# First attention with merged window triangles: half as many probabilities, both heads normalised by VectorE in one multiplication

## What is computed

```python
q = rms_norm(einsum('btd,ndh->btnh', x, q_kernel), q_norm_scale)      # 16 heads of 128
k, v = einsum('bsd,ckdh->cbskh', x, kv_kernel); k = rms_norm(k, k_norm_scale)   # 8 key/value heads
q, k = apply_rope(q, positions), apply_rope(k, positions)
mask = (j <= i) & (i - j < 128)                                       # WINDOW = 128
logits = einsum('btkgh,bskh->bkgts', q * ATTN_SCALE, k)
probs = softmax(where(mask, logits, min))
out = einsum('btnh,nhd->btd', einsum('bkgts,bskh->btkgh', probs, v), out_kernel)
```

## Time and profile before

| | us |
|---|---|
| median of 3 runs | 1585.34 (1585.33 to 1596.49) |
| the profiled execution | 1583.67 |
| its span, first to last instruction | 1581.4 |

### The profile page before, as it was taken

The page is one execution under the profiler, slowest core; times in us unless marked ns, Lnnn a source line. Parts: engine busy times, 40 slices in busy tenths (PEclk is TensorE's granted clock), DMA queues, the critical chain, the costliest instruction groups (busy, mean ns, idle before and its releaser), DMA issues.

```text
span 1581.4 us, 24555 instructions
## 1 busy us (share of the span) xinstructions
PE 1452.6 (92%) x7806; PEld 1104.6 (70%) x7806; DVE 1112.8 (70%) x2356; ACT 810.5 (51%) x1983; POOL 334.4 (21%) x448
## 2 busy tenths in 40 slices
PE   3699999999999999799999999999849898989898
PEld 2589989988998899667777777777624344444376
DVE  5699899989998999377555455455437676767554
ACT  2466676666766767444332332332215464646566
POOL 3364454444444544000000000000012020201000
PEclk9899999999999999899999999999957899999999
DMA  4210000000000000233000000000052232222001
GB/s 130 67 41 1 2 1 1 1 3 1 1 2 1 1 1 1 67 90 90 21 1 0 0 0 0 0 0 0 1 204 65 70 91 70 90 70 90 1 14 40
DMA packets 30796, 52.75 MB, mean 33 GB/s; under 512 B 4480, under 2 KB 12544, under 8 KB 30304
## 3 DMA queue, kind: packets, MB, share of 16 engines
q1 hardware_dynamic: 30288, 50.63, 10.3%
q0 software_dynamic: 400, 0.78, 0.3%
HBM read 37.49 MB, written 14.68 MB: 33 GB/s over the span
## 4 chain that ended last, share of the span: by engine, by line
PE 83%; DVE 7%; ACT 4%; issue 3%; DMA 2%; POOL 0%; SPq 0%; DVEq 0%; ACTq 0%; POOLq 0%
PE ps L1216 16%; PE ps L1218 15%; PE ps L1217 15%; PE ps L1254 6%; PE ps L1300 6%; PE ps L1491 4%; PE ps L1530 4%; PE ps L1331 3%; PE ps L1281 2%; PE ps L1618 2%; PE ps L1504 2%; PE ps L1367 1%; PE ps L1636 1%; PE ps L1292 1%; PE ps L1516 1%
## 5 line engine op out<-in xcount | busy, mean ns | idle before, releaser
L806 DVE TENSOR_REDUCE nm<-ps 128x1 f32<-128x512 f32 x256 | 167.6, 684 | 101.8 <-PE ps L1491 101.7
L1138 ACT ACTIVATE pT<-ps 128x512 f32<-128x512 f32 x256 | 145.9, 597 | 140.0 <-PE ps L1504 137.6
L1216 PE MATMUL ps<-xnT_lo,w1moe_hi 128*128 128x512 f32 x400 | 177.0, 443 | 4.7 <-DVE w2moe_lo L764 4.5
L399 POOL TENSOR_TENSOR ln_rs<-ln_ve,minus_half 128x4 f32<-128x4 f32 x12 | 13.6, 1131 | 775.2 <-DVE ln_ve L496 775.2
L1068 ACT ACTIVATE moe_act_hi<-sg 128x512 fp32r<-128x512 f32 x100 | 63.3, 633 | 191.0 <-DVE sg L741 191.0
L1217 PE MATMUL ps<-xnT_hi,w1moe_lo 128*128 128x512 f32 x400 | 160.5, 401 | 0.0
L1218 PE MATMUL ps<-xnT_hi,w1moe_hi 128*128 128x512 f32 x400 | 159.9, 400 | 0.0
L1216 PE MATMUL ps<-wqkv_lo,xnT_hi 128*128 128x512 f32 x256 | 128.1, 500 | 25.5 <-DVE wqkv_lo L549 25.5
L998 ACT ACTIVATE rope<-ps 128x384 f32<-128x384 f32 x128 | 62.9, 491 | 156.4 <-PE ps L1218 155.4
L731 DVE TENSOR_TENSOR sg<-ps,sg 128x512 f32<-128x512 f32 x100 | 69.0, 690 | 95.5 <-ACT sg L1088 95.3
L424 POOL TENSOR_TENSOR rope<-rope 128x384 f32<-128x384 f32 x128 | 131.7, 1029 | 0.0
(11 more groups left out here) (205 smaller groups left out, 3688.7 us busy)
## 6 DMA issues: line engine op xcount, KB each, us to landing
copies<-qk_hi SPq DMA_DIRECT2D x32, 256.0 KB
yT<-in_w1moe SPq DMA_DIRECT2D x25, 256.0 KB, 2.6
qst<-copies SPq DMA_DIRECT2D x64, 96.0 KB, 2.2
kst<-copies SPq DMA_DIRECT2D x64, 96.0 KB, 2.3
x_res<-in_wqkv SPq DMA_DIRECT2D x8, 512.0 KB, 3.7
copies<-qk_lo SPq DMA_DIRECT2D x16, 256.0 KB
w_in<-in_w2moe SPq DMA_DIRECT2D x25, 128.0 KB, 2.7
x_res<-in_wo SPq DMA_DIRECT2D x4, 512.0 KB, 3.8
```

What stands on the lines that cost most here:

```text
L806: V.tensor_reduce(nm1[:, n % 2, t, col:col + 1], ps[:, 1 + s1_slot(p), :], AX.X, ALU.max, negate=True).then_inc(s1_max, 1)
L1138: A(pT1[:, u % 2, 2 * (m % 2) + h, c, :], ps[:, 4 + e % 2, :], ACT.Exp, scale=SCALE1).then_inc(p1_ready, 1)
L1216: MM(out, left[0], right[1], start=first, stop=False)
```

## The change

For the groups that see two tiles (96 of 128 steps):

- the scores of both tiles are written side by side in PSUM as before, but with no mask matmul; VectorE then copies the older tile's scores over the newer tile's where j > i (`copy_predicated` with an int32 mask `older`, 2 x 128 columns in PSUM, with a one-element memset ahead of it). Maximum, exponentials, normalisation and transposes then work on 2 x 128 columns instead of 2 x 256. Groups of tile 0 keep a mask matmul (`causal`, 256 columns).
- the transposed probabilities (2 x 128 columns) are parted again by GpSimd with two `affine_select`s over 256 elements each: zeros in one copy where the newer tile holds, in the other where the older holds (`parted`, 4 slots). The two products with v take these. In the hardware loop a one-element addition (`idle`) stands ahead of them. `part_probT` runs ahead of L420 in GpSimd's step, for the group of seven steps ago.

For all groups: VectorE normalises both heads in one multiplication with the two reciprocals broadcast (2 x 128 columns); ScalarE's L1014 is gone. On VectorE the order is now reciprocal, merge, normalisation, low part of the output, maximum. The product with v, the output's parts and the output projection come one step later (n - 9, n - 10; LAST_LAG = 10).

At the start: chunk 1 is loaded ahead of the tables, ScalarE and VectorE split two chunks before the first step and then chunk n + 2 ahead of step n; VectorE makes the rope tables of tile 0 only, GpSimd those of the tiles 1 to 3 behind its steps 0 to 2, and its splits of wo come one step sooner (behind steps 6 to 9). `prob` now lies in the memory of yT, so the first exponential also waits for the tables.

The diff, cut to its core:

```diff
-KV_RING, PROB_RING = 2 * GROUPS, 4
-LAST_LAG = 9
+OLDER_STEPS = STEPS - GROUPS
+K_RING, V_RING, PROB_RING, PART_RING = 2 * GROUPS, 4 * GROUPS, 4, 4
+LAST_LAG = 10
...
-        window = sb("window", [P, 2, 2, P], BF16, part_a)
+        idle = sb("idle", [P, 1], where=part_a)
+        causal = sb("causal", [P, 2, P], BF16, part_a)
+        older = sb("older", [P, 2, P], I32, part_a)
...
-        prob = sb("prob", [P, PROB_RING, 2, 2 * P], where=part_a)
+        prob = yT[:].rearrange("p a (b h f) -> p (a b) h f", b=2, h=2)
+        probT = sb("probT", [P, 2, 2, P], where=part_a)
+        parted = sb("parted", [P, PART_RING, 2, 2, P], where=part_a)
...
             load_chunk(0)
+            load_chunk(1)
...
+            sp.dma_start(older[:], dram["c_older"]).then_inc(older_loaded, 16)
+            for j in range(2, STAGES):
...
+            def part_probT(b, n, new, old):
+                m = n - 7
+                if (new if m >= 0 else old) and not alone(m):
+                    kb, s, r = b * STEPS + m, m % 2, m % PART_RING
+                    pool.wait_ge(probT_ready, kb + 1)
+                    if old or m >= PART_RING:
+                        pool.wait_ge(attended, kb - PART_RING + 1)
+                    if not isinstance(b, int):
+                        nc.gpsimd.tensor_tensor(idle[:], minus_half[:, 0:1], minus_half[:, 0:1], ALU.add)
+                    nc.gpsimd.affine_select(parted[:, r, 0], probT[:, s], [[0, 2], [-1, P]], ALU.is_gt, 0.0,
+                                            base=0, channel_multiplier=1)
+                    nc.gpsimd.affine_select(parted[:, r, 1], probT[:, s], [[0, 2], [1, P]], ALU.is_ge, 0.0,
+                                            base=0, channel_multiplier=-1).then_inc(probT_parted, 1)
             def attention_step(b, n, old, following):
+                part_probT(b, n, True, old)
...
+            def tables(t):
+                h2 = HD0 // 2
+                three = lambda table, half: table[:, t:t + 1, half].to_broadcast((P, 3, half.stop - half.start))
+                nc.gpsimd.tensor_tensor(cos3[:, t], three(cos_in, slice(0, HD0)), qks[:], ALU.mult).then_inc(tables_ready, 1)
+                nc.gpsimd.tensor_tensor(sin3[:, t, :, 0:h2], three(sin_in, slice(0, h2)), qks[:, :, h2:HD0], ALU.mult
+                                        ).then_inc(tables_ready, 1)
+                nc.gpsimd.tensor_tensor(sin3[:, t, :, h2:HD0], three(sin_in, slice(h2, HD0)), qks[:, :, 0:h2], ALU.mult
+                                        ).then_inc(tables_ready, 1)
             tile_rms(0, 0)
+            pool.wait_ge(scales_ready, 2)
             for n in range(STEPS):
                 attention_step(0, n, False, True)
-                if GROUPS <= n + 1 < CHUNKS:
-                    split_wo(n + 1)
+                if n + 1 < TT:
+                    tables(n + 1)
+                if GROUPS <= n + 2 < CHUNKS:
+                    split_wo(n + 2)
...
+            for n in range(LAST_LAG):
+                part_probT(BATCHES, n, False, True)
...
-            for h in range(3):
-                sc = qks[:, h:h + 1, :].to_broadcast((P, TT, P))
-                lo, hi = sc[:, :, 0:H2], sc[:, :, H2:HD0]
-                V.tensor_tensor(cos3[:, :, h, :], cos_in, sc, ALU.mult).then_inc(tables_scaled, 1)
-                V.tensor_tensor(sin3[:, :, h, 0:H2], sin_in[:, :, 0:H2], hi, ALU.mult).then_inc(tables_scaled, 1)
-                V.tensor_tensor(sin3[:, :, h, H2:HD0], sin_in[:, :, H2:HD0], lo, ALU.mult).then_inc(tables_scaled, 1)
-            dve.wait_ge(tables_scaled, 11)
+            def turned_in(table, half):
+                return table[:, 0:1, half].to_broadcast((P, 3, H2))
+            V.tensor_tensor(cos3[:, 0], cos_in[:, 0:1, :].to_broadcast((P, 3, P)), qks[:], ALU.mult
...
+            split_wqkv(1)
+            dve.wait_ge(tables0_ready, 3)
...
-                    if old or m >= 2:
-                        dve.wait_ge(normed[1], k - 1)
                     V.reciprocal(rsums[:, s, :], psums[:, s, :]).then_inc(inv_ready, 1)
-                    dve.wait_ge(inv_ready, k + 1)
-                    V.tensor_tensor(prob[:, m % PROB_RING, 0, 0:w], prob[:, m % PROB_RING, 0, 0:w],
-                                    rsums[:, s, 0:1].to_broadcast((P, w)), ALU.mult).then_inc(normed[0], 1)
                 m = n - 4
                 if valid(m):
-                    k, s, w = k0 + m, m % 2, seen(m)
+                    k, s = k0 + m, m % 2
+                    bank = ps[:, 3 + s, :].rearrange("p (h a f) -> p h a f", h=2, a=2)
                     dve.wait_ge(scored, k + 1)
-                    V.tensor_reduce(nmax[:, s, :], ps[:, 3 + s, :].rearrange("p (h f) -> p h f", h=2)[:, :, 0:w],
-                                    AX.X, ALU.max, negate=True).then_inc(max_ready, 1)
+                    if not alone(m):
+                        V.memset(spare[:, 1:2], 0.0)
+                        V.copy_predicated(bank[:, :, 1, :], older[:], bank[:, :, 0, :]).then_inc(merged, 1)
+                m = n - 6
+                if valid(m):
+                    k, s = k0 + m, m % 2
+                    dve.wait_ge(inv_ready, k + 1)
+                    V.tensor_tensor(prob[:, m % PROB_RING], prob[:, m % PROB_RING],
+                                    rsums[:, s, :].unsqueeze(2).to_broadcast((P, 2, P)), ALU.mult).then_inc(normed, 1)
+                m = n - 9
+                if valid(m):
+                    k, s = k0 + m, m % 2
+                    dve.wait_ge(enc_high, k + 1)
+                    V.tensor_tensor(enc[1][:, s, :], ps[:, 6, 0:2 * P], enc[0][:, s, :], ALU.subtract
+                                    ).then_inc(enc_split, 1)
+                m = n - 4
+                if valid(m):
+                    k, s = k0 + m, m % 2
+                    bank = ps[:, 3 + s, :].rearrange("p (h a f) -> p h a f", h=2, a=2)
+                    if not alone(m):
+                        dve.wait_ge(merged, b * OLDER_STEPS + with_older(m))
+                    V.tensor_reduce(nmax[:, s, :], bank[:, :, 1, :], AX.X, ALU.max, negate=True).then_inc(max_ready, 1)
...
-                m = n - 8
-                if valid(m):
-                    V.tensor_tensor(enc[1][:, s, :], ps[:, 6, 0:2 * P], enc[0][:, s, :], ALU.subtract
...
+                if 2 <= n + 2 < GROUPS:
+                    split_wqkv(n + 2)
                 attention_step(0, n, True, False, True)
-                if n + 1 < GROUPS:
-                    split_wqkv(n + 1)
...
             split_chunk(0)
+            split_chunk(1)
...
-                    kt = slice(0, 4) if seen(m) > P else slice(1, 4, 2)
-                    A(probT[:, s, kt, :], ps[:, 5, :].rearrange("p (a f) -> p a f", a=4)[:, kt, :], ACT.Copy
-                      ).then_inc(probT_ready, 1)
-                m = n - 8
+                    if old or m >= 3:
+                        act.wait_ge(probT_parted, b * OLDER_STEPS + with_older(m - 2))
+                    A(probT[:, s], ps[:, 5, 0:2 * P].rearrange("p (h f) -> p h f", h=2), ACT.Copy).then_inc(probT_ready, 1)
...
-                    act.wait_ge(inv_ready, k + 1)
-                    A(prob[:, m % PROB_RING, 1, 0:w], prob[:, m % PROB_RING, 1, 0:w], ACT.Copy, scale=rsums[:, s, 1:2]
-                      ).then_inc(normed[1], 1)
...
-                        ins = A(prob[:, m % PROB_RING, h, 0:w], ps[:, 3 + s, h * 2 * P:h * 2 * P + w], ACT.Exp,
+                        ins = A(prob[:, m % PROB_RING, h, :], ps[:, 3 + s, (2 * h + 1) * P:(2 * h + 2) * P], ACT.Exp,
...
+                if n + 2 < CHUNKS:
+                    split_chunk(n + 2)
                 attention_step(0, n, True, False, True)
-                if n + 1 < CHUNKS:
-                    split_chunk(n + 1)
...
-                    k, s = k0 + m, m % 2
-                    pe.wait_ge(probT_ready, k + 1)
+                    k, r = k0 + m, m % PART_RING
+                    if alone(m):
+                        pe.wait_ge(probT_ready, k + 1)
+                    else:
+                        pe.wait_ge(probT_parted, b * OLDER_STEPS + with_older(m))
                     if old or m >= 1:
                         pe.wait_ge(enc_split, k)
-                    parts = (0, 1) if seen(m) > P else (1,)
-                    for part in parts:
-                        ins = MM(ps[:, 6, 0:2 * P], v0[:, (m if part else m - GROUPS) % KV_RING, :],
-                                 probT[:, s, part::2, :], start=part == parts[0], stop=part == 1, skip_group_check=True)
+                    if alone(m):
+                        ins = MM(ps[:, 6, 0:2 * P], v0[:, m % V_RING, :], probT[:, m % 2].rearrange("p h f -> p (h f)"),
+                                 start=True, stop=True, skip_group_check=True)
+                    else:
+                        for part in range(2):
+                            ins = MM(ps[:, 6, 0:2 * P], v0[:, (m if part else m - GROUPS) % V_RING, :],
```

(29 more changed lines are left out.)

74 lines of the change are left out of this document (40 added, 34 removed).

## The result

The changed kernel takes 1531.31 us in the median of four runs (1530.54 to 1534.58), the kernel before beside it 1587.1; the ratio is 0.9635, interval 0.9597 to 0.9673. That is 56 us less, where 37 less were forecast. The profiled execution took 1530.54 us, its span 1528.8; TensorE's granted clock is 0.956 (0.958 before).

The account below looks back on a forecast made before the run. TensorE was taken to pace two-tile steps, VectorE single-tile ones, and a GpSimd-VectorE loop the changed two-tile steps. Two-tile -28, single-tile +4, start -15, end +2 make -37: 1585.3 to 1548 us, range 1530 to 1636.

Parts of the forecast that it names:

- What bounds the kernel: First attention: TensorE paces the 96 two-tile steps (4.84 us), VectorE the 32 single-tile ones (3.96 us).
- TensorE's part: Two-tile steps: mask product and two of four transposes go, 4.84 to 4.40 us, 4.45 with the tile's own transposes.
- ScalarE's part, the maximum, copy_predicated: Two-tile steps: ScalarE's lighter work buys nothing; maximum 0.68 to 0.41 us; new copy 0.40 us, covered by GpSimd's rotation.
- The selects: GpSimd, two-tile steps: each of two new affine_selects takes 0.75 us, between ends of 0.23 and 1.23.
- The loop with the selects: VectorE and GpSimd, two-tile steps: loop of 4.52 us, step taken as 4.55 instead of 4.84, 28 us gained.
- The start: Steps 0 to 7: splitting weights two steps ahead opens a chain, 39 instead of 55.5 us; 15 us gain taken.
- Single-tile steps +4: 32 single-tile steps: VectorE's normalisation grows from 128 to 256 elements, 0.13 us a step, 4 us lost.
- end +2: End of the first attention: one more step of lag adds one short drain step, 2 us lost.
- rival 2: Selects of 0.3 to 0.55 us leave no port wait, TensorE stays the bound at 4.45: -46, 1539 us; chance 0.17.
- the forecast itself: Selects of 0.6 to 0.85 us interleave with VectorE's L598: 1548 us, own range 1535 to 1565; chance 0.38.
- Rival 3: Two-tile step does not gain: both selects run ahead of waiting L598, or step stays near 4.8; 1569 to 1601; chance 0.17.
- Rival 4: GpSimd becomes the bound with selects of 1.22 us: loop 5.46 us, 1636 us; decides from 0.96 us; chance 0.28.

Follow-up runs that it names:

- experiment 3: The changed kernel with 512 columns of mask product put back on TensorE in each of the 96 two-tile steps: 1544.91 us.
- experiment 5: The changed kernel with head 1 normalised by ScalarE again and only head 0 by VectorE: 1533.5 us.
- experiment 6: The changed kernel with GpSimd's two selects replaced by two multiplications with 0/1 masks: 1537.85 us.
- experiment 7: The changed kernel with two mask multiplications for the selects and the one-element addition ahead of them in every batch, not only the looped ones: 1530.08 us.
- experiment 8: The changed kernel with the two selects replaced by two TENSOR_SCALARs that copy without parting: 1580.88 us, ratio 0.9955 to the kernel before.

## Why the prediction was right and wrong

**What bounds the kernel: right for the two-tile steps, wrong for the others.** The steps of 3.96 us were read as VectorE's pace because no bracket stood there. But in the kernel before TensorE was busy without a gap there too:

```profile
440.00:570.00 130.00, 129.75 (x856) 116.59 (x855) 120.04 (x283) 90.31 (x287) 60.37 (x89) 1.00 0.01 1
```

(From 345 to 620 us, nearly two batches, it was busy for 274.43 of 275.) VectorE falls behind in the single-tile steps and catches up in the others; what counts is TensorE's sum over 32 steps. That sum fell by 24 x 0.44 = 10.6 us, and the batches got 9.4 to 9.5 shorter. 0.4 of the difference are the two steps in which the mask product had only filled a wait for ScalarE's L1070 (experiment 3), and 0.3 to 0.4 are TensorE's new wait for L580, in one step of 4.51 to 4.57; some 0.3 stay open.

**TensorE's part: right.** 4.40 us, with 4.82 once per tile, as forecast (4.40, 4.45 in the mean).

**ScalarE's part, the maximum, copy_predicated: right.** The copy took 0.42 us (0.40 taken) and lies in the cover of the rotation; the maximum took 0.41; giving ScalarE its half back moved the end of the attention by 0.5 us, 2.0 without the turn (experiment 5).

**The selects: mis-sized.** 0.41 us alone, 0.45 in the mean, where 0.75 was taken; 0.23 and 1.23 were the ends. The value leaned on the two-input operations as the most frequent kind on this engine, which says nothing of a one-input one. With a price of about 0.65 (experiment 6) the whole would have been 1538, so this term is worth some 6.5 us at most; with the addition in every batch (experiment 7) it is worth nothing that can be measured. The Trainium skill, GPSIMD Engine Reference, section 4.1, gives one-input work roughly line rate. From the page's clock of 1.2 GHz that would be an estimate of 0.21 us for 256 elements and a fixed part. For affine_select the trace comes near it (0.36 us start to start); with one size measured, no run here parts the rate from the fixed part. For TENSOR_SCALAR, 1.22 us in experiment 8 where nothing held it, the trace does not bear it out.

**The loop with the selects: the step that failed.** It gave 4.52 us. The one run whose instructions cost about what it assumed (experiment 6, looped batch) had 4.09. The 0.43 are: the add, counted at 0.15 in a row, runs while the port is held and is over 0.01 us behind it (0.14); a multiplication holds the queue for 0.67, twice (0.16); L671 keeps the second one waiting for 0.34, counted from the end of the first, and not 0.47 (0.13). Durations were added where distances from start to start count, although the section on the profile says which of them an instruction costs. The forecast then took 4.55, over TensorE's 4.45, and with that made GpSimd and VectorE the bound of the two-tile steps, at a gain of 28 us. In the changed kernel their loop takes 4.08, also with multiplications of 0.66 in place of the selects (experiment 7), TensorE's step 4.40, and TensorE stays the bound: about 37 us from the two-tile steps. That the unrolled batches of experiment 6 show the very 4.52 is chance: there GpSimd stands idle for 0.95 us ahead of L447, where the forecast's loop has no gap.

**The start: right in its mechanism, 3 us short.** 18.1 gained, 15 forecast; step 8 came at 54.79, forecast 56 to 60. The steps 0 to 7 took 39.2 us, forecast 39; step 0 came 1.8 us sooner, where up to 1 later was feared. The steps with the tables took 4.96, 5.42 and 4.17 us where 5.2 each were taken. That GpSimd's splits of wo "only move" was right: 5.6 us in each of four steps.

**Single-tile steps +4, end +2: not paid.** The steps did get 0.12 longer (4.08 for 3.96, 0.13 forecast), but TensorE's sum sets the batch. From step 127 to the last addition it is 25.9 us for 25.2, +0.7. There, in the drain, TensorE does wait for the parted probabilities, four times and 1.9 us in all, which the prediction had named as a sign against it; in the steps before it does not.

**The sum.** What came true is rival 2, short selects with TensorE as the bound, put at -46 and 1539 with a chance of 0.17; the forecast itself had 0.38. The measured time lies just inside the stated range, at its lower end, but for the reasons of rival 2 and not for those of the forecast. Against it: start 3.1 more, single-tile steps 4 more, end 1.3 more, the rest of the program 1.9 worse, -52.5; the spans differ by 52.6. Rival 3 had in it what the unrolled batches of experiment 6 show, a held L671. Rival 4 had the right bound for its price and the wrong sum (4.98 for 5.46), and its break-even of 0.96 us lay too low: it carried the upper end of the range to 1636, where the same price measured 1581.

## What to carry over

When an engine shows no gap over a whole period, count the period: steps in which another engine is the later one cost nothing as long as the sum of the first stays. Build a loop through a shared resource from start-to-start distances, not from durations, and check which of two instructions arrives first there: 0.05 us ahead or 0.10 behind decided over 0.45. And load and prepare weights two steps ahead where the preparation sits behind the work that it feeds; here that alone was worth 17 us.

## What the runs showed of the hardware

- An affine_select over 2 x 128 columns of fp32 takes 0.41 us on GpSimd; a multiplication of 256 elements with two SBUF inputs 0.66; a TENSOR_SCALAR with two operand scalars 1.22.
- GpSimd's instructions differ in whether they keep VectorE's two-input operations waiting. TENSOR_TENSOR does: L639 takes 1.03 instead of 0.42 beside the rotation. affine_select does, too, as VectorE's and GpSimd's rows of the changed kernel at 240 us show:

```profile
240.19 0.75 DVE L664 TENSOR_TENSOR qkn<-rope,rms 128x384 f32<-128x384 f32 x1
...
240.13 0.40 POOL L435 TENSOR_SCALAR_AFFINE_SELECT parted<-probT 128x256 f32<-128x256 f32 x1
240.49 0.72 POOL L437 TENSOR_SCALAR_AFFINE_SELECT parted<-probT 128x256 f32<-128x256 f32 x1
```

- L664 ends 0.41 us behind the first select's end, and the second is longer by 0.31. TENSOR_SCALAR does not (experiment 8): L639 keeps its 0.42 inside it, and L664 its 0.54 where it starts 0.55 us into one. It waits itself, though, for a L664 that started 0.10 us before it (1.56 instead of 1.22). The Trainium skill, SBUF — State Buffer, section "SBUF: two separate sides", says that a VectorE operation with two SBUF inputs and a GpSimd one that reads SBUF exclude each other for the whole instruction. The first two kinds agree with it; for TENSOR_SCALAR the measurement decides against it in one direction, since VectorE's operation never waits.
- A one-element addition ahead of the contended instruction made the steps 0.43 us shorter (experiments 6 and 7).
- The turn of the hardware loop cost some 2 to 5 us, which differ between executions of the same kernel (steps 63 and 64: 12.59 and 10.99 us, two ordinary ones 8.8).
